# Queries and keys projected once and doubled through DRAM, in a one-core attention and mixture-of-experts layer

## What is computed

```python
q = silu(x @ Wq); k = silu(x @ Wk); v = x @ Wv      # 16 heads of 8 features
q = concat([q * cos(theta * n), q * sin(theta * n)], -1)   # per head, 8 -> 16 features
k = concat([k * cos(theta * n), k * sin(theta * n)], -1)
out = ((q @ k.T) * causal_mask) @ v                 # no softmax
out = (out @ Wo) * sigmoid(x @ G1 @ G2)
x1 = layernorm(x + layernorm(out) * gamma + beta)
# then: a shared gated FFN, and 8 experts (top 2 of 8, capacity 1280), and
y = layernorm(x1 + shared(x1) + routed(x1))
```

## Time and profile before

| | us |
|---|---|
| median of three runs | 992.25 |
| the profiled execution's own time | 985.05 |
| its span, first to last instruction | 983.3 |
| TensorE (PE) busy | 915.9 (93%) |
| VectorE (DVE) busy | 566.2 (58%) |
| ScalarE (ACT) busy | 303.1 (31%) |
| DMA moved | 59.21 MB, 60 GB/s over the span |

### The profile page before, as it was taken

One profiled execution on the slowest core, in us unless ns is written; L12 is line 12 of the kernel. 1 busy time (PEld: TensorE's weight loads), 2 busy tenths in 40 slices (PEclk: granted clock), 3 DMA queues, 4 the chain that ended last, 5 costly groups with the idle time before them and its releaser, 6 DMA issues. The chain is left out here.

```text
span 983.3 us, 25364 instructions
## 1 busy us (share of the span) xinstructions
PE 915.9 (93%) x10102; PEld 749.4 (76%) x10102; DVE 566.2 (58%) x1851; ACT 303.1 (31%) x643; POOL 381.1 (39%) x362
## 2 busy tenths in 40 slices
PE   4998999999999999999999899758999999999996
PEld 3676787877778788777778666646999999988885
DVE  5465847566584756657575767743444444435652
ACT  6222323223231323223232212112333333235563
POOL 4004233140413224041322443354587887771220
PEclk8797999999999999999999978759999999999998
DMA  4413111020111102021121212103345554344331
GB/s 117 146 37 128 35 34 45 25 54 24 54 24 45 43 26 54 25 57 22 42 52 37 58 46 48 34 23 109 77 87 99 88 91 62 38 43 133 108 107 33
DMA packets 74197, 59.21 MB, mean 60 GB/s; under 512 B 10147, under 2 KB 64218, under 8 KB 74080
## 3 DMA queue, kind: packets, MB, share of 16 engines
q1 hardware_dynamic: 57312, 41.58, 15.3%
q0 software_dynamic: 16768, 16.01, 9.1%
HBM read 23.47 MB, written 28.89 MB: 53 GB/s over the span
## 5 line engine op out<-in xcount | busy, mean ns | idle before, releaser
L507 POOL DMA_INDIRECT dispatched_rows<-x,slot x128 | 126.2, 986 | 60.6 <-issue 39.5
L534 POOL DMA_INDIRECT summed_rows<-VP,goal_i x80 | 123.7, 1546 | 46.7 <-DVE VP L1030 24.0
L806 DVE TENSOR_TENSOR EM<-energy_banks,causal 128x512 f32<-128x512 f32 x128 | 87.6, 684 | 41.0 <-PE energy_banks L1152 41.0
L479 POOL TENSOR_TENSOR rr<-vq,minus_half 128x8 f32<-128x8 f32 x16 | 26.2, 1638 | 214.9 <-DVE vq L949 214.9
L1113 PE MATMUL bank<-xgT_hi,ws_hi 128*128 128x512 f32 x216 | 97.5, 451 | 10.6 <-DVE he L832 8.4
L832 DVE TENSOR_TENSOR he<-sf,bank 128x512 f32<-128x512 f32 x88 | 60.4, 686 | 81.2 <-PE bank L1115 63.2
L592 ACT ACTIVATE sf<-bank 128x512 f32<-128x512 f32 x88 | 52.6, 598 | 145.2 <-PE bank L1115 144.7
L1171 PEld LDWEIGHTS bank<-VP,Kt 64*128 64x128 f32 x448 | 61.4, 196 | 39.5 <-issue 37.4
L1227 PE MATMUL bank<-sd_s,he 128*128 128x128 f32 x704 | 84.2, 278 | 6.1 <-DVE he L832 6.1
L1115 PE MATMUL bank<-xgT_hi,ws_lo 128*128 128x512 f32 x216 | 87.5, 405 | 0.0
L1114 PE MATMUL bank<-xgT_lo,ws_hi 128*128 128x512 f32 x216 | 87.5, 405 | 0.0
(11 more groups left out here) (180 smaller groups left out, 1760.5 us busy)
## 6 DMA issues: line engine op xcount, KB each, us to landing
QM<-QT SPq DMA_DIRECT2D x256, 32.0 KB, 2.0
dispatched_rows<-empty POOLq DMA_DIRECT2D x8, 655.0 KB
QM<-dispatched_rows SPq DMA_DIRECT2D x8, 655.0 KB, 5.7
xin<-in_x SPq DMA_DIRECT2D x16, 256.0 KB, 3.0
QM<-summed_rows SPq DMA_DIRECT2D x16, 256.0 KB, 2.8
out_x<-QM SPq DMA_DIRECT2D x16, 256.0 KB, 2.3
summed_rows<-empty SPq DMA_DIRECT2D x11, 256.0 KB, 2.0
dispatched_rows<-x,slot POOLq DMA_INDIRECT x128
```

What stands on the lines that cost most here:

```text
L507: g.indirect_dma_start(out=xg_d, out_offset=bass.IndirectOffsetOnAxis(ap=slot[:, par, j:j + 1], axis=0), in_=x1[:, par, j % NC, :], in_off ...
L534: g.indirect_dma_start(out=sum_d, out_offset=bass.IndirectOffsetOnAxis(ap=goal_i[:, par, t:t + 1], axis=0), in_=ye[:, par, t, :], in_offse ...
L806: v.tensor_tensor(EM[:, c % 2, i], EB2[:, i].rearrange("p (h n) -> p h n", h=8), causal[:].unsqueeze(1).broadcast_to([P, 8, T]), ALU.mult) ...
```

## The change

Queries and keys are projected once, each into one tile of 128 rows, silu is applied once, and the activated tile is doubled on its way through DRAM: stored twice into interleaved rows of a DRAM tensor and read back as two tiles. One buffer of `QM` is left, filled in halves. TensorE's projections i = 2 and 3 and their silus are gone, all four turns stand together, and SP gets two `double` calls a step: for the queries at the head of the step, for the keys ahead of the spreading. The waits that projections 2 and 3 had for their banks move to the projection of the values.

```diff
+        qk_d = nc.dram_tensor("qk_rows", [2, 2 * P, S], f32, kind="Internal").ap()
-        wqk_hi, wqk_lo = we_hi[:, 1, 0], we_lo[:, 1, 0]
+        wqk_hi, wqk_lo = we_hi[:, 1, 0, 0:2 * P], we_lo[:, 1, 0, 0:2 * P]
+        dq = sb("dq", [P, 2, 2, S])
-        QM = sb("QM", [P, 2, 2, 2, 2, 4, P])
+        QM = sb("QM", [P, 2, 2, 2, 4, P])
...
# SyncE
+            def double(f, kind):
+
+                sp.wait_ge(a_silu, 2 * f + kind + 1)
+                for rows in (0, 1):
+                    sp.dma_start(qk_d[kind].rearrange("(h i d) n -> i h d n", i=2, d=8)[rows], sq[:, kind]).then_inc(st_qk, 16)
+                sp.wait_ge(st_qk, 64 * f + 32 * kind + 32)
+                need(sp, v_qk, 4 * (f - 1) + 2 * kind + 2)
+                sp.dma_start(dq[:, kind], qk_d[kind].rearrange("(t p) n -> p t n", p=P)).then_inc(d_qk[kind], 16)
+
             def step(b, par):
+                if within(b, -1, 14):
+                    double(b + 1, 0)
                 if within(b, 0, 13):
...
                 if within(b, -1, 14):
+                    double(b + 1, 1)
                     if b == -1:
-                        sp.wait_ge(z_qm, 2)
+                        sp.wait_ge(z_qm, 1)
                     need(sp, v_qk, 4 * b + 6)
-                    need(sp, pe_E, 8 * b)
                     for g2 in (0, 1):
+                        need(sp, pe_E, 8 * b + 4 * g2 + 4)
                         for h in range(8):
...
# ScalarE
-                need(act, pe_qk, 4 * f + i + 1)
-                need(act, v_qk, 4 * f + i - 1)
+                need(act, pe_qk, 2 * f + i + 1)
+                need(act, st_qk, 64 * (f - 1) + 32 * i + 32)
...
-                    clear(flat(QM)[:, 32 * P:64 * P], 32 * P).then_inc(z_qm, 1)
...
-                if front:
-                    silu(f, fp, 2)
-                    silu(f, fp, 3)
# VectorE
-            link(v.tensor_copy(wqk_hi, sq[:, 0]))
-            link(v.tensor_tensor(wqk_lo, sq[:, 0], wqk_hi.bitcast(f32), ALU.subtract))
+            single = sq[:, 0].rearrange("p (h i d) -> p h i d", i=2, d=8)[:, :, 0]
+            hi, lo = (w.rearrange("p (h d) -> p h d", d=8) for w in (wqk_hi, wqk_lo))
+            link(v.tensor_copy(hi, single))
+            link(v.tensor_tensor(lo, single, hi.bitcast(f32), ALU.subtract))
...
-                need(dve, a_silu, 4 * f + i + 1)
+                need(dve, d_qk[i // 2], 16 * (f + 1))
...
                 shared_hidden(b, 1)
-                if front:
-                    turn(f, fp, 0)
...
                 if front:
-                    turn(f, fp, 1)
-                    turn(f, fp, 2)
-                    turn(f, fp, 3)
+                    for i in range(4):
+                        turn(f, fp, i)
                 shared_hidden(b, 4)
# TensorE
                 shared_pair(3)
-                if front:
-                    project(f, 2)
-                    project(f, 3)
                 shared_pair(4)
                 if front:
                     for i in (0, 1):
-                        need(pe, a_silu, 4 * f + 3 + i)
+                        need(pe, a_silu, 2 * f + 1 + i)
+                        need(pe, (v_y, v_lg)[i], f - 1 - i)
```

More of the change, by code:

```diff
@@ L166, in build @@
         ac = flat(QM)[:, 0:NB * NC * P].rearrange("p (i c d) -> p i c d", i=NB, c=NC)
-        x1t = flat(QM)[:, 60 * P:64 * P].rearrange("p (c d) -> p c d", c=NC)
+        x1t = flat(QM)[:, 24 * P:28 * P].rearrange("p (c d) -> p c d", c=NC)
         expert = sb("expert", [P, 1])
@@ L217, in build @@
         g_qm = (sem("q_by_head_first"), sem("q_by_head_second"))
+        st_qk = sem("qk_stored"); d_qk = (sem("q_doubled"), sem("k_doubled"))
         sp_x1 = sem("sums_stored"); xs_free = sem("sums_kept")
@@ L345, in step @@
                 if within(b, -1, 14):
+                    double(b + 1, 1)
                     if b == -1:
-                        sp.wait_ge(z_qm, 2)
+                        sp.wait_ge(z_qm, 1)
                     need(sp, v_qk, 4 * b + 6)
-                    need(sp, pe_E, 8 * b)
                     for g2 in (0, 1):
+                        need(sp, pe_E, 8 * b + 4 * g2 + 4)
                         for h in range(8):
                             rows = slice(16 * h, 16 * h + 16)
-                            sp.dma_start(QM[rows, 1 - par, g2, :, :, h % 4].rearrange("p t c n -> p (t c) n"),
+                            sp.dma_start(QM[rows, g2, :, :, h % 4].rearrange("p t c n -> p (t c) n"),
                                          QT[rows, 1 - par, g2].rearrange("p t (c n) -> p (t c) n", c=2)).then_inc(g_qm[g2], 16)
@@ L562, in silu @@
             def silu(f, par, i):
[L563 to L564 removed]
+                need(act, pe_qk, 2 * f + i + 1)
+                need(act, st_qk, 64 * (f - 1) + 32 * i + 32)
                 if f == 0 and i == 1:
                     act.wait_ge(c_dve, 8)
[L567 removed]
+                a.activation(sq[:, i], PB[i][:], ACT.Silu).then_inc(a_silu, 1)
             def copy_out(b, c, par):
@@ L795, in turn @@
                     need(dve, g_qm[1], P * (f - 1))
-                activated, angles = sq[:, i % 2], table[:, i % 2]
+                activated, angles = dq[:, i // 2, i % 2], table[:, i % 2]
                 if i < 2:
@@ L1153, in energies @@
                                                KT[rows, par, t2, P * c + T * s:P * c + T * (s + 1)],
-                                               QM[rows, par, c // 2, t2, c % 2, :, tok], start=True, stop=True)
+                                               QM[rows, c // 2, t2, c % 2, :, tok], start=True, stop=True)
                                 if t2 == 1 and s == 1:
@@ L1284, in step @@
                     need(pe, a_out, 4 * b)
-                    need(pe, a_silu, 4 * last(b + 1) + 1)
+                    need(pe, a_silu, 2 * last(b + 1) + 1)
                     need(pe, v_y, b - 1)
@@ L1294, in step @@
                     need(pe, a_x1T, b - 1)
-                    need(pe, a_silu, 4 * last(b + 1) + 2)
+                    need(pe, a_silu, 2 * last(b + 1) + 2)
                     for c in range(NC):
```

6 lines of the change are left out of this document (removed).

## The result

The changed kernel takes 1041.9 us in the median of four runs (1038.7 to 1046.8), the kernel before, run beside it, 993.3 us (992.2 to 995.2): a ratio of 1.049, 95% interval 1.045 to 1.054, about 49 us slower. The forecast was 1023 us with a range of 1004 to 1054. The profiled execution of the changed kernel is its slowest, 1046.8 us with a span of 1045.1, and that of before lies under its runs (985.05 us, span 983.3), so the two traces are 61.8 us apart where the medians are 48.7. I explain the traces' 61.8 us and keep in mind that a part of them differs from execution to execution: the mean granted clock is 0.897 in the profiled execution and 0.906 to 0.907 in the three others of the changed kernel.

A forecast was written before the change was run, and what follows sets the result against it. In FFN steps DVE's gapless second half, not PE at 93% busy, was taken as the bound; 2.3 + 18.4 + 4.6 + 3 + 2 + 0.6 = +30.9 us on 992.25 gave about 1023 us, range 1004 to 1054.

The forecast's parts named there:

- PE relief gives nothing: Projections 2 and 3 removed: 22 us of PE time, but in steps 2 to 11 it releases only FFN piece 4.
- Rival (a): All steps: relief of PE pays, 992 - 22 = 970 us; chance 0.05.
- Four turns for three, +0.23 us an FFN step: DVE, steps 2 to 11: piece 4 starts at 283.32 instead of 283.09, 10 x 0.23 = +2.3 us.
- The FFN steps' cover of about 1 us: Steps 2 to 11: key data there at about 281.0, key turns at 282.1, so the trip is covered by about 1 us.
- rival (c): FFN steps: keys late there too with a trip longer by 3 us, about 1052 us; chance 0.13.
- The trip's own length: Trip through DRAM: about 7.4 us from the end of the silu to the data, bounds 6.4 and 10.
- Steps 12 to 14, the chain of landings: SP's landing waits make the keys late by 8.4, 6.0 and 4.0 us, together +18.4, bounds +10 and +30.
- Rival (b): Steps 12 to 14: the trips are hidden even there, about 993 us, no change; chance 0.07.
- The clock, +4.6 in step 13 alone: PE idle about 7 us in step 12 drops step 13's granted clock: +4.6 us, bounds 0 and 14.
- The start and steps 0 and 1, +5.6: Late query and key data: start +3 (0 to 6), step 0 +2 (0 to 5), step 1 +0.6 (-1 to 3).
- rival (d): FFN steps: PE's new waits let the clock fall in each, 10 x 4.6 more, 1069 us; chance 0.07.
- No wait before the key turns: Sign for the FFN steps: DVE has no wait before the key turns; a DMA wait there would mean rival (c).

The follow-up runs named there:

- the hybrid: Trip only for fronts made in steps 2 to 11, query turns early; four doubled projections elsewhere, one buffer; against the kernel before: 1079.9 us against 1091.0, ratio 0.987.

## Why the prediction was right, and where it was too small

The sign, the places of the loss and the range were right; the point was 19 us low, because the key waits and above all the clock were sized too small. By its steps:

- **PE relief gives nothing.** Right, and shown by the kernel without a trip, on its chip. Rival (a) is out.
- **Four turns for three, +0.23 us an FFN step.** Measured +0.18 a step on the first chip (1.66 over nine, in which the two late keys are), 0.04 on the others. Right.
- **The FFN steps' cover of about 1 us.** Right in sign, too good in size: the margin is about nothing (waits of 0.17 and 0.42 us in two of nine steps, up to 1.6 in the hybrid), so of the sign of rival (c), a DMA wait at the turns, a trace is there. The FFN sum's store was composed at 4.9 us from its issue with the queue ahead of it and took 4.4 in step 6. What was off is the key stores: composed 3.3 us, they took 4.91 in step 6 and 4.11 in step 3. Rival (c) needed 3 us more and got none of its 10 x 2.
- **The trip's own length.** Stores 1.2 and landing: composed 3.3 us from issue, measured 3.56 for the keys of step 12 and 4.29 for the queries; load composed 3.65 after its issue, median 3.7. The Trainium skill's estimate of 3.2 us for the load (page "DMA: Bandwidth & Descriptors", section "Anatomy of one DMA"), which holds for another issuing path, lies 0.5 under the measured median. The prediction's "some 3 us smaller" applied it to the loads alone; for a 256 KB store the same formula gives an estimate of 2.6 us where 2.1 was composed, and the trip comes out as long as before.
- **Steps 12 to 14, the chain of landings.** Right in its links, 21.2 us from the query stores' issue to the key turn in step 12 where the composition gave 18.8 from the end of the silu. x1's landing, 5.3 us after the issue of both stores against 3.8 composed, is the largest error. The key waits grew by 10.1, 8.4 and 5.5 us where 8.4, 6.0 and 4.0 were forecast, 24.0 in place of 18.4. Rival (b) is out.
- **The clock, +4.6 in step 13 alone.** This is the term of the sum that was mis-sized most in the late steps. A fall was priced once, from one step that lasts 32 us in place of 27, and in step 13 that price held: the step is 12.7 us longer, 8.4 of it the key wait and 4.3 the rest. But the clock is low through step 15 too, which by itself is 9.6 us longer at 0.50 instead of 0.80. I had written "step 14 has its fall already" and not looked beyond the last step that has a wait. Of the 15.2 us by which steps 12 to 15 came out over the forecast in this pair of traces (38.2 against 23.0), 9.6 stand in step 15 and 5.6 are longer key waits. On the slower chips, where step 15 costs nothing, these steps lost 20.2 us, near the forecast.
- **The start and steps 0 and 1, +5.6.** Measured +23.0 in the trace. The start (+5.1) was within its bounds (0 to 6); step 0 (+8.2) and step 1 (+9.7) were outside theirs (to 5 and 3). That the keys of step 0 come late was called harmless because the next step begins with the spreading. But the spreading stands behind the key doubling on SP, the key turns wait 6.34 us behind it and PE 2.67 for them, and the row "step 1" had no room for a clock fall: it was at 1.00 before and is at 0.63. The slower chips show as much, 21.2 us up to step 2 against 20.3 here, so this part is no chance of one execution. As much of the miss lies here (17.4 us, less 2.8 that step 2 gives back) as in the late steps.
- **Clock falls in the FFN steps, rival (d).** Didn't happen on the first chip; every slice of the page has 9 there, and energies take 1.09 us.

The signs that the prediction named came in the main as named (an FFN step of 43.7 us; PE's idle time ahead of shared_down 2.0 us in step 6 where 2.4 was named; DMA waits at the third turn in steps 12 to 14, though of 7 to 12 us, not 4 to 9; the clock of step 13 low, 0.67 where 0.8 was named). "No wait before the key turns" in the FFN steps failed in two of nine. Not settled: how many of the 49 us are clock and how many are wait. The one run meant for it held the clock in two steps only and paid for it. In the late steps of the traces the key waits account for 24.0 of 38.2 us on the first chip and 17.7 of 20.2 on the slower ones; that the rest is clock is an estimate.

## What to carry to other kernels

Ask of a removed instruction which half of the step it stands in and who the next consumer waits for; an engine busy for 93% of the span gave nothing back here until the other engine's work moved as well. A DMA round trip costs not only its landings but everything that stands behind its waits in the issuing queue: put waits for landings behind all issues that somebody needs. And when a change adds a wait on TensorE, follow the granted clock past the end of the wait, and look at another execution before you price it: of the late steps' clock one pair of traces here made 9.6 us in a step without any wait, another made 0.4.

## What the runs showed of the hardware that was not expected

The same program takes 993 to 995 us on two chips and 1091 to 1093 us on three others. The waits of PE in the FFN steps show a part of it; kernel before, other chip:

```profile
PE bank L1195 <- issue: 22.3, 32, 1.2
```

PE waits for nothing that the profile shows, 32 times at the matmuls of attend alone in the stretch from 158 to 560 us; on the first chip the stretch from 108 to 499 has no such row for PE matmuls. An FFN step lasts 51.15 us there and 43.52 here, and the granted clock of the stretch is 0.93 in place of 1.00. The row above makes up 2.8 of the 7.6 us a step; about half of the 7.6 is longer busy time of PE at the lower clock (46.9 us a step where it is 43.0 on the first chip). What makes PE's instructions late on those chips no run here tells. For a study it means that gains in us do not carry over: the same change costs 4.9% on one chip and 3.7% on another.
